# Messages of a graph layer in fewer, wider items: 8 of 20 chunks instead of 10 of 16

## The reference

```python
x = x + gnn(_layernorm(x), edge_attr, path_coeffs, src, dst, path_indices)
x = x + ffn(_layernorm(x), Wr, sWg, sWu, sWd, Wg, Wu, Wd)

# gnn: 20000 edges sorted by dst, 16 segments of 32 values, 64 paths (i1, i2, i3)
x1 = x_nodes[src].reshape(-1, 16, 32)
x2 = x_edges.reshape(-1, 16, 32)
contrib = path_coeffs[None, :, None] * x1[:, i1, :] * x2[:, i2, :]
edge_out = zeros(E, 16, 32).at[:, i3, :].add(contrib)
out = zeros(625, 512).at[dst].add(edge_out.reshape(-1, 512))

# ffn: 2 shared experts on all rows, 64 experts of 512x512x512 (SwiGLU), top 6 per row
out = shared + routed + x
```

## Time and profile before

| | us |
|---|---|
| median of three runs | 1057.06 |
| the profiled execution | 1064.52 |
| its span (first to last instruction) | 1063.3 |
| VectorE busy | 567.7 |
| TensorE (PE) busy | 885.2 |
| ScalarE (ACT) busy | 232.5 |
| GpSimd (POOL) busy | 333.4 |

### The profile page before, as it was taken

How to read it: one execution, slowest core, us unless ns; L and a number is a source line. 1 busy time by engine, 2 the same in 40 slices (tenths; PEclk the granted TensorE clock), 3 DMA queues, 4 the chain that set the end, 5 groups by cost and what they waited for, 6 DMA issues and landing times.

```text
span 1063.3 us, 20703 instructions
## 1 busy us (share of the span) xinstructions
PE 885.2 (83%) x7145; PEld 483.9 (46%) x7146; DVE 567.7 (53%) x1347; ACT 232.5 (22%) x589; POOL 333.4 (31%) x388
## 2 busy tenths in 40 slices
PE   0267768767667768899999999999997999989988
PEld 0134434334333334585454544646444445445455
DVE  6799999999999998576211111121111221211216
ACT  1332222223222221231211111111210211111100
POOL 4554433523523510023323232233232232322120
PEclk9999899899999999799999999999998999999999
DMA  8857557656755743946999999999999999999928
GB/s 249 326 170 248 201 196 238 223 188 224 245 191 200 262 174 121 346 160 236 384 390 392 394 394 397 389 395 387 397 395 405 380 395 392 394 392 390 392 78 321
DMA packets 70230, 320.41 MB, mean 301 GB/s; under 512 B 12892, under 2 KB 13045, under 8 KB 48200
## 3 DMA queue, kind: packets, MB, share of 16 engines
q1 hardware_dynamic: 48175, 261.07, 64.1%
q0 software_dynamic: 21248, 56.55, 16.7%
q10 hardware_dynamic: 665, 0.85, 0.3%
HBM read 308.55 MB, written 12.93 MB: 302 GB/s over the span
## 4 chain that ended last, share of the span: by engine, by line
PE 64%; DVE 17%; issue 9%; DVEq 8%; ACT 1%; DMA 1%; POOL 0%; ACTq 0%; POOLq 0%
PE ps L1313 21%; DVE big L634 12%; PE ps L1371 11%; PE ps L653 9%; PE ps L920 7%; DVEq L632 4%; PE ps L1248 4%; PE ps L947 3%; DVEq L625 3%; PE ps L1345 2%; PE ps L1306 2%; PE ps L1365 1%; DVEq L634 1%; PE ps L970 1%; DMA big<-in_src 1%
## 5 line engine op out<-in xcount | busy, mean ns | idle before, releaser
L634 DVE TENSOR_TENSOR big<-big 128x512 f32 (+1 forms) x640 | 383.8, 672 | 2.6 <-DMA big<-xn_d,idx 2.6
L653 PE MATMUL ps<-big,mixed 128*32 128x256 f32 x2512 | 169.2, 409 | 128.4 <-DVE big L634 128.4
L1313 PE MATMUL ps<-big 128*64 128x512 f32 x1024 | 237.1, 605 | 18.4 <-issue 17.4
L345 POOL DMA_INDIRECT big<-xn_d,idx x151 | 149.4, 989 | 204.7 <-PE ps L653 164.0
L653 PEld LDWEIGHTS ps<-big,mixed 128*32 128x32 f32 x2512 | 79.3, 115 | 221.1 <-DVE big L634 151.8
L1205 POOL DMA_INDIRECT big<-h_d,idx x64 | 63.0, 984 | 367.9 <-issue 279.3
L1323 DVE TENSOR_TENSOR mixed<-big,ps 128x256 f32<-128x256 f32 x64 | 26.9, 421 | 270.2 <-ACT big L1320 269.9
L1313 PEld LDWEIGHTS ps<-big 128*64 128x64 f32 x1024 | 69.7, 138 | 142.5 <-issue 138.9
L1371 PE MATMUL ps<-big,mixed 128*64 128x256 f32 x1024 | 124.6, 385 | 0.1
L1274 POOL DMA_INDIRECT y_d<-big,sia x74 | 75.3, 1017 | 118.2 <-DVE big L1384 97.9
L1371 PEld LDWEIGHTS ps<-big,mixed 128*64 128x64 f32 x1024 | 68.0, 137 | 34.2 <-issue 2.9
(11 more groups left out here) (226 smaller groups left out, 679.2 us busy)
## 6 DMA issues: line engine op xcount, KB each, us to landing
big<-in_L_ffn_Wg SPq DMA_DIRECT2D x64, 1024.0 KB, 16.2
big<-in_L_ffn_Wu SPq DMA_DIRECT2D x64, 1024.0 KB, 20.7
big<-in_L_ffn_Wd SPq DMA_DIRECT2D x64, 1024.0 KB, 16.9
big<-in_edge_attr SPq DMA_DIRECT2D x39, 1024.0 KB, 5.8
big<-y_d SPq DMA_DIRECT2D x10, 768.0 KB, 11.8
big<-xn_d,idx POOLq DMA_INDIRECT x151, 3.9
big<-in_L_ffn_sWg SPq DMA_DIRECT2D x2, 1024.0 KB, 10.5
big<-in_L_ffn_sWu SPq DMA_DIRECT2D x2, 1024.0 KB, 13.5
```

The source lines that it names most:

```text
L345: pool.indirect_dma_start(xs[s][:, c, :], None, xn_d[:, :], bass.IndirectOffsetOnAxis(ap=table[:, c0 + c:c0 + c + 1], axis=0)).then_inc(x_ ...
L634: ins = dve.tensor_tensor(pr[k % 2][:, 0:chunks, EXT * p:EXT * (p + 1)], xs[s][:, 0:chunks, ds(o1, EXT)], es[s][:, 0:chunks, ds(o2, EXT)], ...
L653: ins = pe.matmul(edge_bank(k // 2)[WIN * h:WIN * (h + 1), h0:h0 + HP * EXT], onehot[s][:, CW * h + r, :], pr[k % 2][:, CW * h + r, :], st ...
L1313: ins = pe.matmul(bank(k2)[TA * h:TA * (h + 1), :].rearrange("p (w f) -> p w f", w=2), xgT[k2][:, k, 0:TA], gu[:, :, k, W * h:W * (h + 1)] ...
```

## The change

The items hold 20 chunks (CW = 5), so there are 8; the first has 2080 edges in 17 chunks, its last quarter being 160 edges in two chunks of 80 partitions. A part is 4 paths instead of 8 (SPQ = 4 parts to a quarter of the paths, SUB = 16), so that the two product buffers are smaller, and four parts fill a bank. RAW goes from 6 to 10, so the raw groups are 7 and 3 chunks. The order inside an item is spread over the 16 parts. Requests for edges, gathers (two per part instead of three) and expert weights follow the new numbering at the same shares of an item. `place_rows` comes one part before the last instead of at the last. The first item's one-hots are issued ahead of ScalarE's wait for the stores; the router's load and the fill behind them. SP asks for the first item's further edges only when both stores have landed. POOL waits for the selection constants before it gathers for the second item, since temporaries now lie in that slot. Small tables move within memory, and the area for descriptors of POOL's transfers shrinks to 8192 bytes.

```diff
-    CW = 4
+    CW = 5
-    EC0 = CW * FQ + 1
-    RAW = 6
+    RC = -(-REST // P)
+    RL = REST // RC
+    EC0 = CW * FQ + RC
+    RAW = 10
-    HP = PP // 2
-    SUB = 2 * PARTS
+    SPQ = 4
+    HP = PP // SPQ
+    SUB = SPQ * PARTS
...
-                sync.wait_ge(part_ok, until + 2 * h)
+                sync.wait_ge(part_ok, until + 4 * h)
...
-    PER = 3
+    PER = 2
...
     sync.wait_ge(G.sem, g_rest)
+    sync.wait_ge(s_xa, n_xa)
+    sync.wait_ge(s_xb, n_xb)
     load_edges(0, 0, quarters=range(1, QW), short=True)
-    act.wait_ge(s_xa, n_xa)
-    s_wr, n_wr = load(act, "ld_router", ...)
-    act.wait_ge(G.sem, g_const)
-    s_zero, n_zero = load(act, "fill_rows", ...)
...
-                if k <= EC // PER and (p % PER == PER - 1 or p == HP - 1):
-                    dve.memset(opening[...], 0.0)
+                if k <= EC // PER and p % 2 == 1:
+                    dve.memset(opening[...], 0.0)
...
-        h0 = HP * EXT * (k % 2)
+        h0 = HP * EXT * (k % SPQ)
-        if k % 2 == 0 and (k > 2 or not at(t, 0)):
-            pe.wait_ge(evt_ok, PARTS * t + k // 2 - 1)
+        if k % SPQ == 0 and (k >= 2 * SPQ or not at(t, 0)):
+            pe.wait_ge(evt_ok, PARTS * t + k // SPQ - 1)
...
     one_hots(0, 0, lambda c: wdst[:, c:c + 1], chunks=EC0)
+    act.wait_ge(s_xa, n_xa)
+    s_wr, n_wr = load(act, "ld_router", ...)
+    act.wait_ge(G.sem, g_const)
+    s_zero, n_zero = load(act, "fill_rows", ...)
+    sync.wait_ge(x_in[0], 16 * (EC0 - RAW))
+    sync.wait_ge(s_zero, n_zero)
+    load_edges(1, SHORT)
...
     after(dve, V, v_sel)
+    after(pool, V, v_sel)
...
-            q = PARTS * t + k // 2 - 1
-            if q >= 0 and k % 2 == 0:
+            q = PARTS * t + k // SPQ - 1
+            if q >= 0 and k % SPQ == 0:
                 turn(q // PARTS, q % PARTS)
                 evict_turned(q // PARTS, q % PARTS)
-            if q >= 0 and k % 2 == 1:
+            if q >= 0 and k % SPQ == 2:
                 select(q // PARTS, q % PARTS)
-            if k % 2 == 1:
-                evict(t, k // 2)
+            if k % SPQ == SPQ - 1:
+                evict(t, k // SPQ)
-            if t > 0 and k == 1:
+            if t > 0 and k == 2:
                 evict_sums(t - 1)
-            if t > 0 and 2 <= k < 2 + NB:
-                put(t - 1, range(k - 2, k - 1), start=t == 1)
+            b = k // 2 - 2
+            if t > 0 and k % 2 == 0 and 0 <= b < NB:
+                put(t - 1, range(b, b + 1), start=t == 1)
-            if t + 1 < NG and 2 <= k < 6:
+            if t + 1 < NG and k % 2 == 1 and 0 <= b < QW:
                 one_hots(t + 1, 1 - s, ...)
-            if k == SUB - 1:
+            if k == SUB - 2:
                 place_rows(t, nrow[:, t:t + 1])
...
-        sync.wait_ge(part_ok, SUB * (NG - 1) + 3 * t)
+        sync.wait_ge(part_ok, SUB * (NG - 1) + 6 * t)
         load_gate_up(t, t)
-        sync.wait_ge(part_ok, SUB * (NG - 1) + 3 * t + 2)
+        sync.wait_ge(part_ok, SUB * (NG - 1) + 6 * t + 4)
         load_down(t, t)
...
-    nc = _bacc.Bacc("TRN2", target_bir_lowering=False, num_devices=1)
+    nc = _bacc.Bacc("TRN2", target_bir_lowering=False, num_devices=1, dynamic_dma_scratch_size=8192)
```

More of the change, by code:

```diff
@@ L86, in gnn_moe @@
     assert N == NB * BP and TCR <= P
-    assert FQ == QW - 1 and 0 < REST <= P and NG % 2 == 0 and NR <= P
+    assert FQ == QW - 1 and RL * RC == REST > 0 and RC <= CW and NG % 2 == 0 and NR <= P
     def sb(name, shape, dt=F32):
@@ L171, in gnn_moe @@
     desf3 = desf.rearrange("p (b k) -> p b k", b=NB)
[L172 to L177, removed]
+    cb = later(P, E * (MAXB - 1)).rearrange("p (e m) -> p e m", e=E)
+    cnt = later(P, E)
+    cs_ = [later(P, E) for _ in range(6)]
     idx = sb("idx", [P, NR * CW], I32)
@@ L235, in gnn_moe @@
     codes = sb("codes", [BP, NB, TOPK])
-    one1 = sb("one1", [BP, NB * TB])
+    one1 = later(BP, NB * TB)
     oneh = [m.rearrange("p (b r) -> p b r", b=NB)
@@ L239, in gnn_moe @@
     mr = one1[:, 0:NB * (E + 2)].rearrange("p (b e) -> p b e", b=NB)
-    idx_1 = sb("idx_1", [TB, E], I32)
-    gs = sb("gs", [P, 2, E])
+    idx_1 = later(TB, E, I32)
+    gs = later(P, 2 * E).rearrange("p (w e) -> p w e", w=2)
     halfm = sb("halfm", [P, 2])
@@ L245, in gnn_moe @@
     ctab = sb("ctab", [P, 4], I32)
-    crow = sb("crow", [1, TCR * 4], I32)
-    Lg = sb("Lg", [TB, MAXC - E, 4], I32)
-    Ls = sb("Ls", [P, 2, MAXC - E, 4], I32)
+    crow = later(1, TCR * 4, I32)
+    Lg = later(TB, (MAXC - E) * 4, I32).rearrange("p (t c) -> p t c", c=4)
+    Ls = later(P, 2 * (MAXC - E) * 4, I32).rearrange("p (w t c) -> p w t c", w=2, c=4)
     none = [sb(f"none{k}", [2, 4], I32) for k in range(4)]
@@ L252, in gnn_moe @@
     half = sb("half", [P, 2])
-    sia = sb("sia", [P, 2, E], I32)
-    mrow = sb("mrow", [1, E + 1], I32)
+    sia = later(P, 2 * E, I32).rearrange("p (w e) -> p w e", w=2)
+    mrow = later(1, E + 1, I32)
     yall = ring[:, 0:NB * TOPK * D].rearrange("p (b k d) -> p b k d", b=NB, k=TOPK)
@@ L373, in gnn_moe @@
     G(pool.iota(gtab[:, :], pattern=[[GE, NG]], base=SHORT - GE, channel_multiplier=0))
-    G(pool.memset(es[0][:, CW * FQ, :], 0.0))
+    G(pool.memset(es[0][:, CW * FQ:CW * FQ + RC, :], 0.0))
     g_rest = G.n
@@ L423, in gnn_moe @@
     s_dst, n_dst = load_ends("ld_dst", dst_r, dst, V)
-    s_pi, n_pi = load(act, "ld_paths", (praw[:, :], path_indices.rearrange("(a n) c -> a (n c)", a=1)))
+    s_pi, n_pi = load(act, "ld_paths", (praw, path_indices.rearrange("(a n) c -> a (n c)", a=1)))
     cview = path_coeffs.rearrange("(t q) -> q t", q=PP)
@@ L652, in contract @@
                     continue
[L653 removed]
+                ins = pe.matmul(edge_bank(k // SPQ)[WIN * h:WIN * (h + 1), h0:h0 + HP * EXT],
                                 onehot[s][:, CW * h + r, :], pr[k % 2][:, CW * h + r, :], start=r == 0,
@@ L824, in more_item @@
         for qq in range(PARTS):
-            contract(t, 1, 2 * qq, chunks)
-            contract(t, 1, 2 * qq + 1, chunks)
+            for k in range(SPQ * qq, SPQ * (qq + 1)):
+                contract(t, 1, k, chunks)
             evict(t, qq)
```

33 lines of the change are left out of this document (16 added, 17 removed).

## The result

The kernel after takes 1061.64 us in the median (1058.89 to 1063.63, 9 runs), the kernel before on the same chip 1057.06 (1055.18 to 1060.54, 9 runs): ratio 1.0039, interval 1.0025 to 1.0052. It is slower by 4.6 us, where 4.3 us faster was forecast. The profiled execution of the kernel after took 1062.98 us, its span 1061.8.

The account below looks back on a forecast made before the run. VectorE's message products bound the kernel up to 422.5 us, then a chain of small steps, then the experts' weight transfers. Start +3.7, products -8.1, hand-offs +1.3, tail -1.2 gave -4.3: 1057.06 to 1052.8 us, range 1047 to 1058.

Parts of the forecast that it names:

- Products, -8.1: VectorE's message products: 512 instructions instead of 640 for the same columns save 8.1 us; bounds 0 to -18.
- the fixed part of 0.063 us: Part of each VectorE product instruction that doesn't grow with columns, read from start to start; saved 128 times.
- 0.143 us: Rival on VectorE products: the whole fixed duration per instruction counts, -18 in place of -8, about 1043 us; chance 0.02.
- the 5.0 us for memsets and contention: Products' time beyond the instruction sum, put down to tiny memsets and contention; kept unchanged, giving 375.9 us.
- Start, +3.7: First item's start: normalising ten raw chunks instead of six moves the first product to 42.3 us; bounds +0.5 to +8.
- the late-start rival: First item starts at 46 (+3.5 more) because edges or the seventh raw gather are late: 1056.5 us; chance 0.13.
- second root: First item's start: the second root queues behind seven applications on ScalarE, so its answer comes later, +2.7 us.
- Hand-offs, +1.3 (0 to 5): Buffer hand-backs from TensorE to VectorE in the items: shorter parts cost 1.3 us of waits, bounds 0 to 5.
- each hand-off 0.1 us late, +13: Weaker form of the rival that TensorE takes VectorE's place: about 1066 us; both forms together 0.12.
- Tail, -1.2: Behind the products: shorter last contraction saves 0.6 us, the placement matrix coming one part earlier saves 0.6.
- Register load: First item's start: loading half as many offset registers takes 0.8 us instead of 1.10, -0.3 (0 to -0.5).
- A shift of the products' end passes through to the end one for one: Stages behind the products: weight slots come free as expert items consume them, so the end moves equally.

Follow-up runs that it names:

- e2: Kernel after with 128 plain TensorE nops in the jumped-over stretch, which were dropped, so a repeat of the kernel after: 1083.65 us, ratio 1.0228.
- e5: Kernel after, unchanged, on another chip: 1079.09 us, ratio 1.0188.
- e6: Kernel after with 128 plain nops that were dropped, so again the kernel after, on the same chip as e5: 1079.69 us, ratio 1.0207.
- e9: Kernel after with 80 signalling TensorE nops in the jumped-over stretch, moving the jump's target to 10 behind a piece's start: 1053.48 us, ratio 0.9958.
- e12: Kernel after with 80 jumped-over signalling nops and an item's 20 gathers spread over 14 of its 16 parts: 1053.59 us, ratio 0.9958.
- e14: Kernel after with 80 jumped-over signalling nops, as e9, on a chip that makes signals late: 1072.57 us, ratio 1.0141.
- e15: Kernel after with 80 jumped-over nops and gathers spread over 14 parts, as e12, on the chip of e16: 1058.0 us, ratio 0.9981.
- e16: Kernel after, unchanged, on a third chip: 1082.36 us, ratio 1.021.
- e8: Kernel after with 6 chunks gathered raw instead of ten (RAW = 6): 1078.7 us, ratio 1.02.
- e11: Kernel before with only the descriptor area of POOL's transfers cut from 16384 to 8192 bytes: 1058.69 us, ratio 1.0011.
- e1: Kernel before, unchanged, run again for a trace near its median: 1058.37 us, ratio 0.9996.
- e13: Kernel before with 168 jumped-over signalling TensorE nops, moving the jump's target to 10 behind a piece's start: 1060.12 us, ratio 1.0002.
- e10: Kernel before with 88 jumped-over signalling TensorE nops, moving the jump's target to 70 ahead of the next piece: 1069.04 us, ratio 1.0104.
- e3: Kernel after with items of 16 chunks (CW = 4) and six gathered raw, keeping its order and parts of 4 paths: 1108.76 us, ratio 1.0488.

## Why the prediction was wrong, point by point

- **Products, -8.1:** the price is right. From start to start 0.74 us for the 0.737 worked out, so the fixed part of 0.063 us holds; 0.143 us does not. The 376.25 us hold 3.4 us of waits; without them 372.9 remain for 375.9, as the 5.0 us for memsets and contention, kept over from before, were some 3 us too many.
- **Start, +3.7:** right in the execution shown (42.65 against 38.6), by luck. It is the earliest of the nine traces with the change's start (after, e2, e5, e6, e9, e12, e14, e15, e16: 42.7 to 48.5, mean 45.4); the five with that before have 36.6 to 39.1, mean 38.2. In the mean the step is +7.3, so the late-start rival is real. The second root does stand behind seven applications, as worked out, but the whole chain often runs later (its answer is used at 38.85 in after, at 44.67 in e16).
- **Hand-offs, +1.3 (0 to 5):** within its bounds for the result, as VectorE waited 3.4 us for TensorE; a contraction took 1.30 us for the 1.35 worked out. Too narrow for the kernel: on three of the four chips of the experiments the products take 13 to 18 us more (389.5 to 394.2 us in e2, e5, e6, e8, e14 and e16). I reasoned from durations of work, and took a signal to be there when the work is done. That is the rival "each hand-off 0.1 us late, +13", by another mechanism than the one I gave it.
- **Tail, -1.2:** right: products' end to the last of `put` is 9.8 us for 11.2 in e11.
- **Register load:** 0.60 us for eight, where 0.8 was taken.
- **"A shift of the products' end passes through to the end one for one":** this is the step that failed. It holds only if the stages behind run as before. With the tail's -1.2 the forecast was -1.2 up to the experts, 0 in their stream, 0 behind; measured from e11 to after are +3.4, +2.2 and +5.1 (against e1 and e13 as before: +2.0 and +1.6, +2.8 and +0.2, +4.0 and +3.7), in sum 10.7 us more for 1.2 less. From e11 to e9, the kernel after with the target moved, they are -0.2, +1.9 and +1.7. So the first and the last are the layout's, and the 2 us in the stream are no more than single executions of the kernel before differ by (560.2 to 562.8).

Of the +5.1 behind the stream 2.7 us are the stall. The other 2.4 go with the granted clock, 0.90 in that stretch against 0.98 in e11: the 128 matmul records of `keep_clock` there are busy for 16.9 us for 14.55. The clock stood at 1.2 GHz from 1026.4 to 1033.2, after TensorE had been idle for 2.55 us and, six matmuls later, again; in e11, idle once for 2.11 us, it stayed at 2.4 GHz there.

What the change did is make TensorE's program 6232 instructions longer ahead of that target: 4776 in the items, which write out more and smaller contractions, and 1456 in the leftover items, which this input never executes. That is 24 pieces and 88 instructions, so the target stands 70 instead of 158 ahead of the next piece. The sum had no term for this. Nor had the range: even both upper bounds together (start +8, hand-offs +5) give +3.7, or 1060.8 us, and the range stopped at 1058.

Where signals are in time, the change at equal layout is worth about what was forecast. With both kernels' targets 10 behind a piece's start the ratios are 0.9958 (e9) and 1.0002 (e13), so -0.44%; with both 70 ahead, 1.0039 and 1.0104, so -0.64%. Forecast was -4.3 of 1057, -0.41%. In part this is luck: in e9 the start is 5.0 us later than in e11 (3.7 forecast) and the products are 9.4 us shorter, waits included (6.8 forecast). Where signals are late, it costs: e14 against e13, at the same layout and on one chip, is 1.4% slower.

The jump is where a rule of the Trainium skill bears: "Runtime: NRT & Kernel Launch", section "Instruction fetch mechanics", says that code arrives in blocks of 16 KiB (256 instructions), that a taken branch out of the current window waits for a fetch, and that crossing a block's edge is mostly hidden. The traces agree with the block and the first wait (the jump takes 5.9 to 6.6 us in every kernel here, also before). They differ on the last point right behind a jump: the edge cost 3.44 us in after and 3.49 in e10 (2.0 to 3.7 in nine traces).

What stays open: by what path a gather holds back TensorE's signal, and why only some chips show it; whether the smaller descriptor area adds to the late signals (55 of 128 in e5 with it, 22 of 80 in e1 without); where in the experts' stream e10 loses 3 to 5 us; and why the start moves by 6 us from one execution to another.

## What to carry to other kernels

When a change alters how much code stands in a stretch that is jumped over, look for idle time with the releaser "issue" at the same count of instructions behind a long jump, in the kernels before and after: it is layout, not the change, and a few dozen signalling nops in the skipped stretch move it. Move it in both kernels before comparing them, since 88 such nops alone made a kernel 1% slower. A hand-off is safe only by the margin between the signal and the need for it: before halving a part, ask what could make the signal late, and try the kernel on more than one chip. Pacing indirect gathers one by one instead of back to back costs nothing where signals are in time (e12) and gave 1.6% where they are not (e15).

## What the runs showed of the hardware

- After a long jump TensorE's second packet of instructions comes 5.7 to 6.0 us behind the first (6.5 once, in e14), whether the code in between is used up or not (427.68 and 433.49 in after, 432.61 and 438.55 in before); in after work goes on 1.4 us after it has landed. With 31 recorded instructions between, the stall is 3.44 us (2.0 to 3.7 in nine traces), with 39 it is 1.77 (e3), and in the kernel before, whose target is 88 further from the edge, there is none.
- A semaphore update of TensorE can be seen 0.3 to 2.7 us after the instruction that gives it (up to 3.5 in e3, 4.0 once in e13), while GpSimd issues indirect gathers back to back; 0.04 us is normal. The first runs of the kernel after and the chip of e9 to e12 showed none.
- Behind the jump at the end of the stream, 80 and 88 instructions that never run go with 3.4 us less (39.2 to 35.8) and 6.0 us more (34.1 to 40.1; the other kernels before have 35.2 and 35.5). The stall is 2.0 to 2.9 us of this, the granted clock behind it the rest (1.2 GHz for 6.8 us in after, 10.2 in e10, 3.4 in e9).
